# Products whose result is not read, queued on TensorE in the gaps of three barriers

## The reference

```python
x = x + L0_ffn(L0_cond(x, cond_8, ...), ...)       # a linear map with LoRA parts, layer norm,
                                                   # 8-bit fake quantization, ternary product
x = x + L1_ffn(L1_cond(x, cond_8, ...), ...)       # 2 of 8 experts and a shared expert (gelu),
                                                   # then the quantized gated product below
def L1_ffn(x):
    x    = act_qdq(x)                               # scale = max|x| of the whole tensor / 32767
    up   = act_qdq(x @ W_up.T)
    gate = act_qdq(x @ W_gate.T)
    gate = act_qdq(gate * round_u16(sigmoid(gate)))
    o    = act_qdq(gate * up)
    return o @ W_down.T
```

## Time and profile before

| | us |
|---|---|
| median of 3 runs | 483.24 (483.06 to 489.1) |
| the profiled execution, its own time | 483.56 |
| its span, first to last instruction | 481.8 |
| TensorE busy in products | 383.0 (79%) |
| TensorE's share of the chain of work that ended last | 63% of the span |
| VectorE busy | 336.4 (70%) |
| ScalarE busy | 272.2 (56%) |
| GpSimd busy | 249.8 (52%) |
| mean granted TensorE clock | 0.911 of full speed |

### The profile page before, as it was taken

One profiled execution on the slowest core, in us unless ns is written; L12 is line 12 of the kernel. 1 busy time (PEld: TensorE's weight loads), 2 busy tenths in 40 slices (PEclk: granted clock), 3 DMA queues, 4 the chain that ended last, 5 costly groups with the idle time before them and its releaser, 6 DMA issues.

```text
span 481.8 us, 8531 instructions
## 1 busy us (share of the span) xinstructions
PE 383.0 (79%) x2556; PEld 337.8 (70%) x2556; DVE 336.4 (70%) x569; ACT 272.2 (56%) x411; POOL 249.8 (52%) x440
## 2 busy tenths in 40 slices
PE   2998759899999999999999999999587950000297
PEld 2776536599999999999999987777355630000297
DVE  2598468667797676767777766469376779979653
ACT  2576568654545455454545446766366679568360
POOL 1575627677686665756564015554242029957130
PEclk9999969999999999999999999999789985555599
DMA  8989910377777767677776309000000000000012
GB/s 269 361 283 329 303 76 1 103 259 254 245 263 232 278 220 285 231 262 246 249 263 237 115 23 340 11 0 1 0 0 0 1 0 0 1 0 0 0 67 109
DMA packets 31651, 71.27 MB, mean 148 GB/s; under 512 B 3571, under 2 KB 19702, under 8 KB 26614
## 3 DMA queue, kind: packets, MB, share of 16 engines
q1 hardware_dynamic: 28982, 66.33, 39.7%
q0 software_dynamic: 1152, 4.19, 2.3%
q10 hardware_dynamic: 1472, 0.20, 0.3%
HBM read 55.12 MB, written 15.60 MB: 147 GB/s over the span
## 4 chain that ended last, share of the span: by engine, by line
PE 63%; DVE 17%; ACT 9%; POOL 4%; issue 2%; DMA 2%; POOLq 1%; ACTq 0%; DVEq 0%
PE ps L180 46%; PE ps L735 11%; DVE S L198 8%; DVE G L189 4%; PE ps L738 4%; PE ps L177 2%; DMA wbr<-in_L_cond_W_base_dram 2%; ACT G L186 2%; ACT ps L186 1%; POOL Hl L189 1%; POOL XCl L189 1%; ACT C_i L186 1%; ACT U L186 1%; ACT xnT L186 1%; DVE xnT L189 1%
## 5 line engine op out<-in xcount | busy, mean ns | idle before, releaser
L690 POOL CAST xg<-XT 128x64 fp32r x312 | 114.7, 415 | 55.8 <-PE ps L180 50.5
L180 PE MATMUL ps<-xg,Wr 128*128 128x256 f32 x936 | 120.2, 284 | 1.4 <-POOL xg L690 1.1
L186 ACT ACTIVATE Gb<-ps 128x512 f32<-128x512 f32 x110 | 65.8, 598 | 96.2 <-PE ps L180 95.8
L189 DVE TENSOR_TENSOR HbS<-Gb,ps 128x512 f32<-128x512 f32 x110 | 75.5, 686 | 60.6 <-PE ps L180 58.7
L180 PEld LDWEIGHTS ps<-xg,Wr 128*128 128x128 f32 x936 | 114.2, 190 | 2.0 <-POOL xg L690 1.5
L186 ACT ACTIVATE Hh<-HbS 128x512 fp32r<-128x512 f32 x110 | 69.1, 628 | 13.3 <-DVE HbS L189 13.2
L735 PE MATMUL ps<-WD,Hh 128*128 x312 | 74.3, 328 | 0.0
L738 PE MATMUL ps<-WD,Hl 128*128 x312 | 69.4, 223 | 0.0
L189 DVE TENSOR_TENSOR Hl<-HbS,Hh 128x512 fp32r<-128x512 f32 x92 | 65.8, 722 | 2.8
L738 PEld LDWEIGHTS ps<-WD,Hl 128*128 128x128 f32 x312 | 59.8, 192 | 0.0
L735 PEld LDWEIGHTS ps<-WD,Hh 128*128 128x128 f32 x312 | 59.0, 189 | 0.0
(11 more groups left out here) (183 smaller groups left out, 691.5 us busy)
## 6 DMA issues: line engine op xcount, KB each, us to landing
Wr<-wscr SPq DMA_DIRECT2D x39, 1024.0 KB, 4.9
wscr<-wst SPq DMA_DIRECT2D x16, 512.0 KB, 4.3
yscr<-Yb SPq DMA_DIRECT2D x39, 128.0 KB, 2.7
stg<-n_L_cond_skill_gate_dram SPq DMA_DIRECT2D x8, 256.0 KB, 5.7
stg<-in_L_cond_skill_up_dram SPq DMA_DIRECT2D x8, 256.0 KB, 6.0
wdr<-n_L_cond_skill_down_dram SPq DMA_DIRECT2D x8, 256.0 KB, 5.4
out_dram<-X SPq DMA_DIRECT2D x7, 256.0 KB, 2.0
X<-in_x_dram SPq DMA_DIRECT2D x3, 512.0 KB, 7.0
```

The lines of the kernel that those rows point to most:

```text
L180: return lambda e: e.matmul(o_, l, r, start=start, stop=stop, skip_group_check=True)
L186: return lambda e: e.activation(o_, i_, func, **kw)
L189: return lambda e: e.tensor_tensor(o_, a, b, op)
L690: k_xg[i] = pool.do(lambda e, s=s: e.tensor_copy(xg[:, i % XR, :, T * s:T * s + T], XT[:, :, :, bass.ds(regb[i][s], 1)].rearrange("p a t o ...
```

## The change

A helper `keep_warm(k, B, w_, x_, *waits)` appends k products of 512 columns to TensorE's list. They have start and stop set, write to bank `B` and have no signal; nothing reads what they write. `allmax` gets an optional set of counts: so many such products ahead of `turn_max`, between `turn_max` and `spread_max`, and behind `spread_max`. At the first maximum the counts are 12, 1 and 7, at the maximum of C 7, 1 and 8, at the maximum of o 0, 0 and 4. At the maximum of o three more are queued ahead of `turn_max`, with a wait for `d_near` (the last reduction on VectorE but one) and for the PSUM slot; two more wait for the ScalarE operation of the second piece of block 0, one for that of its third piece. No other instruction is changed.

```diff
--- before.py
+++ after.py
@@ -509,11 +509,23 @@
         def spread_max(B, k, d_):
             return pe.do(mm(B[:, 128:129], S4[0:1, 40:41].broadcast_to([1, 128]), S4[0:1, 41 + k:42 + k], True, True), d_, d_one)
 
-        def allmax(src, B, k, d_):
-
-            return spread_max(B, k, top_max(B, k, turn_max(src, B, d_)))
-
-        k_ = allmax(S[:, 180:181], bank[6], 0, d_)
+        def keep_warm(k, B, w_, x_, *waits):
+            for _ in range(k):
+                pe.do(mm(B, w_, x_, True, True), *waits, sig=False)
+
+        def allmax(src, B, k, d_, *busy):
+
+            def warm(i):
+                if busy:
+                    keep_warm(busy[0][i], *busy[1:])
+            warm(0)
+            p_ = turn_max(src, B, d_)
+            warm(1)
+            p_ = spread_max(B, k, top_max(B, k, p_))
+            warm(2)
+            return p_
+
+        k_ = allmax(S[:, 180:181], bank[6], 0, d_, (12, 1, 7), bank[2], WbTh[:, :], xTh[:, 0, :])
         d_ = dve.do(ts(S[:, 182:183], bank[6][:, 128:129], 1e-8, 1.0 / 127, ALU.max, MUL), k_)
         dve.do(lambda e: e.reciprocal(S[:, 183:184], S[:, 182:183]), d_)
         d_sa = dve.do(tt(S[:, 180:181], S[:, 182:183], S[:, 142:143], MUL), d_)
@@ -871,7 +883,7 @@
             return slice(1024 * p, 1024 * p + 1024)
 
         d_ = dve.do(red(col(TMP), S[:, 184:192], ALU.max), *d_c)
-        k_ = allmax(col(TMP), bank[7], 1, d_)
+        k_ = allmax(col(TMP), bank[7], 1, d_, (7, 1, 8), bank[0], SHh[0][:, 0:128], XT[:, 0, 0:4, :].rearrange("p t b -> p (t b)"))
         d_ = dve.do(ts(col(SX), bank[7][:, 128:129], 1.0 / 32767, 1e-12, MUL, ALU.max), k_)
         d_ix = dve.do(lambda e: e.reciprocal(col(IX), col(SX)), d_)
         d_sxq = dve.do(ts(col(SXQ), col(SX), 1.0 / 32767, None, MUL), d_)
@@ -1023,10 +1035,13 @@
                 d_ = largest_of(Gf, p, OM, o_[p])
                 if len(late) > 1 or p == 11:
                     d_ = largest_of(Gf, late[0], OM, o_[late.pop(0)])
+        d_near = d_
         for p in late:
             d_ = largest_of(Gf, p, OM, o_[p])
+        wx = (bank[0], WFh[:, 0, :], WFh[:, 0:4, :].rearrange("p k c -> p (k c)"))
+        keep_warm(3, *wx, d_near, *fs[0])
         d_ = dve.do(red(col(MX3), S[:, OM:OM + 12], ALU.max), d_)
-        p_ = allmax(col(MX3), bank[7], 5, d_)
+        p_ = allmax(col(MX3), bank[7], 5, d_, (0, 0, 4), *wx)
         d_ = dve.do(ts(col(S3), bank[7][:, 128:129], col(SGR), 1e-12, MUL, ALU.max), p_, d_i3)
         d_ = dve.do(lambda e: e.reciprocal(col(RC), col(S3)), d_)
         d_s = dve.do(tt(col(I3), col(I3), col(RC), MUL), d_)
@@ -1044,6 +1059,8 @@
                 a = act.do(acp(O_i[:, q, cs], G[:, q, cs], ACT.Identity, scale=col(I3)), d_s)
                 eng = pool if j % 2 else dve
                 o_[j] = eng.do(ts(G[:, q, cs], O_i[:, q, cs], 1.0, 0.0, MUL, ADD), a)
+                if j < 1 and q.start:
+                    keep_warm(3 - q.start, *wx, a)
 
         def down_o(j):
             for t in range(4):
```

## The result

The changed kernel takes 480.8 us as the median of 17 runs (477.97 to 484.77), the kernel before in 17 runs beside them 484.59 us (482.26 to 489.1). The ratio is 0.9932, with a 95% interval from 0.9908 to 0.9955: 3.3 us faster (2.2 to 4.5). The forecast was 478.4 us against 483.24 us, a ratio of 0.990 and 4.8 us. The sign is right and the time lies in the forecast range, but the forecast gain of 4.8 us lies outside the measured interval. Ratios and intervals leave out executions more than 1.5% above the fastest of the same kernel.

A forecast was written before the change was run, and what follows sets the result against it. TensorE, 63% of the chain, was taken to lose its full clock at three barriers where it idles. Gains of 1.8 + 1.4 + 1.6 = 4.8 us from 483.56 us give 478.8, with the median 0.32 lower 478.4 us; range 476.0 to 481.2 us.

The forecast's parts named there:

- The cost of the products: First barrier covered, second 0, at most 0.15 us; at the maximum of o 0.45 us lost if the clock is low.
- If the clock stays at 2.4 GHz from 63.5 to 73.77 us: Condition behind the first maximum under which three steps of the chain shorten, by 0.5, 0.6 and 0.7 us.
- rival B: First barrier: clock falls again in the loop, or ScalarE and VectorE take up the gain; 479.7 us, chance 0.13.
- The term of 1.8 us: Gain at the first barrier, the first maximum, with the clock held: 1.8 us, bounds 1.0 and 2.4 us.
- The term of 1.4 us: Gain at the second barrier, the maximum of C: ScalarE starts unit two 1.4 us earlier, bounds 1.0 and 1.6 us.
- Maximum of o: Last products: clock back near 456 us, block 0 ends 1.6 us earlier; bounds -0.45 and 2.2 us.
- Rival A: At the end, the clock comes back no earlier, as waits for VectorE break the row; 480.5 us, chance 0.18.
- D: All three barriers: products don't hold the clock and stand in the way; 1.8 us more, 485.0 us, chance 0.05.
- E: Every barrier: the change does nothing to the clock and costs nothing; 483.2 us, chance 0.03.
- The experts' loop: Sign behind the first barrier: the loop starts 1.8 us earlier, near 94.6 us instead of 96.4 us.
- The second unit's copy: Sign behind the maximum of C: ScalarE's copy of the second unit comes 3.2 us earlier than at 350.89 us.
- The distance from the maximum of C to that of o: Sign for the second barrier's gain: the distance between these two maxima shrinks by 1.4 us.

The follow-up runs named there:

- e1: Kernel before with only the products at the first maximum (12, 1, 7); ratio 0.9952 to the kernel before, 2.3 us faster.
- e6: Changed kernel plus products filling the pauses in the loop behind the first maximum and four waits for XCl; 479.66 us, ratio 0.9895 to the kernel before.
- e8: Changed kernel with the edits of e6 and e7 together; ratio 0.9898 to the kernel before, 4.9 us faster.
- e9: Against e6, at the maximum of o 16 products ahead instead of three, one between, nine behind instead of four; 478.29 us, ratio 0.9851 to the kernel before.
- e2: Kernel before with only the products at the maximum of C (7, 1, 8); ratio 0.9976 to the kernel before.
- e10: Changed kernel with only the four waits for XCl filled, nothing added behind the first maximum; 478.87 us, ratio 0.9865 to the kernel before.
- e5: The changed kernel once more, unaltered, on the chip of e6 to e8; 481.68 us, ratio 0.9922 to the kernel before.
- e7: Changed kernel, at the maximum of o eight products ahead instead of three, one fewer for the second piece, none for the third; ratio 0.9968 to the kernel before.
- e4: Changed kernel with every added product streaming 8 columns instead of 512; ratio 0.9978 to the kernel before.
- e11: The kernel of e4 run once more, all added products with 8 columns; 485.0 us, ratio 0.9994 to the kernel before.

## Why the prediction was right or wrong

- **The cost of the products: right.** The real product behind each of the first two barriers comes where it came (2.83 and 2.88 us behind the turning product, 2.84 and 2.88 us before). At the maximum of o it comes 4.89 instead of 4.46 us behind it: 0.43 us, for the predicted 0.35 to 0.45 us at the low clock.
- **The size of each gain with the clock held: right.** 1.8 us predicted at the first barrier, 1.9 us in e1 and 1.5 to 1.7 us with the pauses filled (e6, e8, e9). 1.4 us at the second, 1.3 us at D2a in e2 and 1.2 us at D2 in e6 and e10. The ten of the result's seventeen executions in which the clock did not fall again (at most 62.3 us low) took 480.1 us on average, 5.0 us below the 485.1 us of the kernel before; the other seven took 482.2 us.
- **The step that failed** is the condition "If the clock stays at 2.4 GHz from 63.5 to 73.77 us", and the same, unsaid, at the second barrier. I costed the products against the barrier, found the barrier covered, and took the clock as held for all that follows. I had the pauses in hand: 66.87 to 69.49 us with four turning products (rival B, 0.13), and the wait up to 347.50 us, which I used only to say that nothing is won before it. At the second barrier I named no rival at all in which the clock falls again. In the changed kernel's profile it fell behind both, at 68.8 and 345.2 us, and once more at 358.9 us, where the kernel before kept the clock in its own profile over the same kind of pause. The term of 1.8 us became 0.9 us there. The term of 1.4 us became -0.9 us there and +0.15 us in e2. That is where the missing gain went: it was won at the barrier and given back behind it.
- **Rival B** was priced by its end result (479.7 us) and came true in its mechanism at the first barrier; it left 0.5 us of that term where 0.9 us were measured, and it was too narrow, since it kept the full 1.4 us of the second. Whether the turning products matter in it, as transposes don't count as busy in the same way by the Trainium skill (TensorE: Matmul & The Clock Gate, Part 4: PE-mode transpose), these runs don't show: e1 held the clock over the same four turning products and the same pause, the profile after didn't, and in e6 other products were put between.
- **Maximum of o: right in mechanism, a little too large in size.** 1.6 us predicted, 1.4 us between the two profiles, 1.0 us between the means of the profiles with and without products. The term compared block 0's addition on VectorE (460.30 us) with an end on TensorE (458.1 us). By the records alone, 19 of them at 4.03 / 19 = 0.212 us instead of 0.112 us, TensorE could win 1.9 us, not 2.2 us. That e9 reached 2.2 us is luck for the number: 1.9 us are the real products, the other 0.3 us the small ones, which the prediction didn't count.
- **Rival A** came about in part in e5 and e10, where the clock came back 2.8 and 2.4 us behind the first real product and D3 gained only 0.2 and 0.4 us. D and E didn't come about in any profile of the whole change. e7 shows A's result (no gain at the end) by another road: a clock that came back too early.
- **Signs that fit by luck.** The experts' loop starts at 94.77 us, near the 94.6 us named, but 0.7 us of it was there ahead of the first maximum. The second unit's copy comes 3.0 us earlier than 350.89 us, for 3.2 us named, but D2a gave only 0.3 us of that. The distance from the maximum of C to that of o, which was to shrink by 1.4 us, grew by 1.0 us: the reading that showed the failed step. The mean clock of about 0.935 was reached in the executions without a further fall (0.935 and 0.936), not in the profiled one (0.925).
- **The spread** was underestimated. I took one trace's low clock as that of the kernel. Over 79 executions the kernel before has 81.6 to 102.7 us of it, and the changed kernel's gain hangs on whether the clock falls again, which differs from execution to execution of the same program. What decides it in one execution stays open.

## What to carry over

Work that only keeps TensorE's clock up should cover the pauses up to the next long busy stretch, not only the one that made the clock fall: here it fell behind pauses of 1.26 and 1.50 us. Read the pauses behind the barrier, in a trace at the full clock, before taking the gain. The number of filling products has to be right for both clocks, as they run out almost twice as fast (0.229 against 0.427 us each) once they have worked; in e9 they started early enough to leave room for that. Judge such a change by the distances between fixed points of several profiles and by the mean clock of every execution; the median of the kernel before went from 483.24 us (3 runs) to 485.68 us (35 runs) here, with nothing changed.

## What had not been expected of the hardware

- The clock fell behind pauses of 1.26 us (344.80 and 358.71 us after; 352.74 us in e2) and 1.50 us (68.30 us after), in stretches in which TensorE was otherwise well busy (5.01 of 6.50 us and 7.35 of 10.15 us in the windows after). The same pauses passed without a fall elsewhere: 1.50 us in e1, 1.26 us at 352.27 us in the profile after, and the waits for XCl of 1.27 and 1.26 us in the kernel before, up to 361.74 and 368.19 us.
- It also fell twice ahead of the first maximum in the profiled execution of e1, the first time where nothing was changed, though the kernel before had it at 1.00 there in its profile, so the barriers are not the only places at which time is lost this way. The second fall reached under the twelve products, which took 3.78 us there instead of 3.00 us. Windows of e1:

```profile
46.70:53.20 6.50, 6.50 (x20) 4.86 (x21) 2.03 (x7) 1.76 (x4) 3.66 (x4) 0.50 0.98 321
60.30:63.30 3.00, 3.00 (x12) 2.71 (x13) 1.51 (x3) 1.14 (x2) 3.00 (x3) 0.50 0.35 137
```

- Products of 8 columns in the same number, 46 of them with their weight loads, did nothing for the clock that e4 or e11 shows.
